# Bank evacuations one step later in a 16-wide attention, and one turn inside a run of value products in a 64-wide one

## The chip, the cores and the metric

The kernel runs on one core of a Trainium2 chip. The metric is the time of one execution on the device, in microseconds; lower is better. A core has a matrix engine (TensorE, PE in the rows), three engines for elementwise work (VectorE or DVE, ScalarE or ACT, GpSimd or POOL), a queue that issues transfers (SP), and a PSUM memory of eight banks into which TensorE writes. Every engine works through its own instructions in the order in which they are written; semaphores hold one engine back until another has done its part.

## The reference

Two layers on 2048 tokens (4 sequences of 512) of width 256, in fp32:

```python
x = x + linear_attention(layernorm(x))          # 16 heads, decaying
x = x + hadamard_ffn(layernorm(x))              # gated, 1024 wide
x = x + attention16(layernorm(x))               # 16 heads of 16, 4 key heads, rope
x = x + attention64_and_experts(layernorm(x))   # 32 heads of 64, causal; then 16 experts, top 4
```

The change touches the third and the fourth line. In both the attention is `softmax(q k^T) v` with rotated queries and keys. The third line, for one sequence n:

```python
q, k, v = x @ Wq.T, x @ Wk.T, x @ Wv.T     # 16 query heads, 4 key and value heads, width 16
q, k = q*cos + rotate_half(q)*sin, k*cos + rotate_half(k)*sin
out = softmax(q @ k.T * 16**-0.5) @ v      # every head on its own
x = x + out @ Wo.T
```

## The kernel before, in words

The order of the work on every engine is written out by hand. The 16-wide attention (the functions called `narrow`) is one loop over numbered steps, `for slot in range(FIRST_SLOT, END_SLOT)`, from -38 to 136, that each engine walks by itself. In a step s of 0 to 127 TensorE first makes two score tiles (L1842, two products of 64x512), then the scores of step s+12 for the maxima (L1855), in odd steps from 3 on the value products (L1867, 8 instructions), then whatever needs bank 6, the only bank for side work (`N_MBANK`). ScalarE begins a step with the two exponentials of that step's score tiles (L1451, 128x512 each); TensorE may write the score tiles of step s+1 once the first exponential of step s is done. VectorE takes the negated maxima (L1079, two a step) and adds them, transposed, into the queries (L1097).

The preparations make the queries and keys of the next sequence, in 4 tiles of 128 tokens, for sequences 1 to 3 beside the steps above; those of sequence 0 run from step -38 on, when there is nothing else. `prepared_at(slot, offset)` says which tile is due: tile t of sequence n starts at step 32n - 38 + 5t, and the offset counts from there. All of these use bank 6 one after the other:

- offset 0: TensorE projects the tile (L1909); ScalarE copies it out (L1484, "the projection's copy").
- offset 1: rope on GpSimd (on VectorE for sequence 0), L499 to L503.
- offset 3: ScalarE writes the high halves (L1462 and L1463, four instructions, "the high parts"), then GpSimd or VectorE the rests.
- offsets 6, 7, 8: TensorE turns the keys and then twice four query tiles (L1898, "the turns"); ScalarE copies each out (L1474: 256 columns for the keys, 512 for the queries).

Before each use of bank 6 TensorE waits (`pe.wait_ge(*emptied)`) until the use before it has been copied out. A next tile starts 5 steps later, so offset 5 of a tile is offset 0 of the next, and its offset 8 is offset 3 of the next. The bank also takes the transposes of the maxima (L1876, in steps 6 and 7 of every 8) and the output projection (L1887, steps 37 and 39 of every 32).

The 64-wide attention runs 32 rounds of 16 slots. The table `WIDE` says what follows a slot's scores (L1773): `turn` transposes probabilities (L1783; VectorE copies the even ones out, ScalarE the odd ones, L1419), `values` multiplies by the values (L1795; after step 3 ScalarE copies the result, L1432), `turn_qk` turns the next round's queries (even numbers, 4 tiles, copied at L1398 to `wide_q`) or keys (odd, 2 tiles, to `wide_k`) in bank 6, and `high` and `low` split them. TensorE waits before a `turn_qk` until the one before has been copied out. ScalarE holds a slot's exponential (L1406) back until the next `turn` or `values` of the table.

Of the kernel before, what the change touches and what calls it, by code (L numbers as in the profile page):

```python
# [74 lines left out]
def two_layers(nc, x_in, slope, W_qkvu, W_out0, SU_ug, SU_dp, Wscale_ug, Wscale_dp, W_up, W_gate, W_down,  # L75
               Wq1, Wk1, Wv1, Wo1, ln_w, ff_ln_w, wq, wk, wv, wo, wg, w1, w3, w2, consts, out):
    ctx = ExitStack()
    with ctx:
# [192 lines left out]
        def n_probs(pair):  # L271

            ring = most_probs[:, 2 * (pair % 6):2 * (pair % 6) + 2, :] if pair % 6 < 4 else \
                more_probs[:, 2 * (pair % 6) - 8:2 * (pair % 6) - 6, :]
            return ring
# [84 lines left out]
        def prepared_at(slot, offset):  # L360

            for n in range(B):
                t, rest = divmod(slot - 32 * n - FIRST_SLOT - offset, 5)
                if rest == 0 and 0 <= t < TB:
                    return n, t
            return None

        def projected_at(slot, offset):
# [13 lines left out]
                9: [("turn_qk", 1, 2), ("turn", 0, 2), ("high", 1, 2), ("qkv", 1, 3)],  # L382
                10: [("low", 1, 2), ("turn_qk", 1, 3), ("turn", 0, 3)],
                11: [("turn", 0, 4), ("high", 1, 3)],
                12: [("low", 1, 3), ("turn", 0, 5), ("values", 0, 0), ("values", 0, 1), ("values", 0, 2), ("values", 0, 3),
                     ("turn_qk", 1, 4)],
                13: [("turn", 0, 6), ("turn_qk", 1, 5)],
                14: [("turn_qk", 1, 6), ("project", 0, 0)],
                15: [("turn_qk", 1, 7), ("values", 0, 4), ("values", 0, 5), ("values", 0, 6), ("turn", 0, 7)]}
# [123 lines left out]
        def narrow_parts(t):  # L513

            whole = n_t1[:, t % 2, :]
            q = whole[:, 0:D].rearrange("p (g i d) -> p i g d", g=KV16, i=4)
            k = whole[:, D:320].rearrange("p (g d) -> p g d", g=KV16)
            qx = n_x[:, t % 2, 0:8, :].rearrange("p (i k) (e w d) -> p i (k e) w d", k=2, e=2, w=4)
            kx = n_x[:, t % 2, 8:10, :].rearrange("p k (e w d) -> p (k e) w d", e=2, w=4)
            return q, k, qx, kx  # L520
# [730 lines left out]
        def _(act):  # L1251
# [191 lines left out]
            def narrow():  # L1443

                for slot in range(FIRST_SLOT, END_SLOT):
                    if 0 <= slot < 8 * SETS:
                        act.wait_ge(n1["sT"], slot + 1)
                        if slot >= 6:
                            act.wait_ge(n1["pv"], (slot - 6) // 2 + 1)
                        for e in range(2):  # L1450
                            nc.scalar.activation(n_probs(slot)[:, e, :], bank[(2 * slot + e) % 3], ACT.Exp).then_inc(n1["exp"], 1)  # L1451
                    at = prepared_at(slot, 3)
                    if at:
                        n, t = at
                        m = TB * n + t
                        q, k, qx, kx = narrow_parts(t)
                        act.wait_ge(n1["sum"], m + 1)
                        act.wait_ge(n1["fill"], 6)
                        if m >= 2:
                            act.wait_ge(n1["turn"], 3 * (m - 1))  # L1460
                        for w in range(2):
                            nc.scalar.activation(kx[:, :, 2 * w, :], k, ACT.Copy)  # L1462
                            ins = nc.scalar.activation(qx[:, :, :, w, :], q, ACT.Copy)  # L1463
                        ins.then_inc(n1["hi"], 1)
                    for i in range(3):
                        at = prepared_at(slot, 6 + i)
                        if at:
                            n, t = at
                            act.wait_ge(n1["turn"], 3 * (TB * n + t) + i + 1)
                            if n >= 2 and t == 0:  # L1470
                                act.wait_ge(n1["sT"], 32 * (n - 1))
                            tiles = n_q[:, n % 2, 4 * (i - 1):4 * i, P * t:P * t + P] if i else n_k[:, n % 2, :, P * t:P * t + P]
                            count = 4 if i else 2
                            nc.scalar.activation(tiles, bank[N_MBANK][:, 0:count * P].rearrange("p (k n) -> p k n", k=count), ACT.Copy,  # L1474
                                                 scale=HD16 ** -0.5 if i else 1.0).then_inc(n1["turned"], 1)
                    at = prepared_at(slot, 0)
                    if at:
                        n, t = at
                        m = TB * n + t
                        act.wait_ge(n1["qkv"], m + 1)  # L1480
                        if m >= 2:
                            act.wait_ge(n1["sum"], m - 1)
                            act.wait_ge(n1["v"], m - 1)
                        nc.scalar.activation(n_qkv[:, t % 2, :], bank[N_MBANK][:, 0:QKV], ACT.Copy).then_inc(n1["q_sb"], 1)  # L1484
# [3 lines left out]


            narrow()  # L1490

            for phase in (3, 4):
# [574 lines left out]
```

## Time and profile before

| | us |
|---|---|
| median of 3 runs | 2081.49 (2073.62 to 2081.84) |
| profiled execution | 2081.78 |
| its span, first to last instruction | 2080.0 |
| TensorE busy in the span | 1802.4 (87%) |
| VectorE busy | 1295.1 (62%) |
| ScalarE busy | 1069.6 (51%) |
| GpSimd busy | 904.0 (43%) |

The mean granted TensorE clock is 0.93 of full speed. The 16-wide attention runs from about 418 to 764 us, its steps 0 to 127 from 479.9 to about 750 us; the 64-wide one, with its rounds, from about 800 to 1709 us. Busy shares are averages over such stages, so the change has to be read inside its own stage. An idle time in a row stands in brackets, with the instruction whose end released it.

### The profile page before, as it was taken

How to read it: one execution, taken by the hardware profiler on the slowest of the kernel's cores; microseconds unless marked ns; L12 is line 12 of the kernel's file. 1: busy time of each engine (PE TensorE's matmuls, PEld its weight loads, DVE VectorE, ACT ScalarE, POOL GpSimd, SP SyncE). 2: the span in 40 equal slices, each digit the busy share in tenths (PEclk: the TensorE clock that was granted, in tenths of full speed). 3: DMA queues.
4: the chain of work that ended last, by engine and by line, in shares of the span. 5: the costliest groups of instructions: out<-in, count | busy, mean ns of one | idle time of the engine just before them, and what ended most of it. 6: DMA issues, size and time to landing. Idle time of an engine off the chain costs nothing.

```text
span 2080.0 us, 32302 instructions
## 1 busy us (share of the span) xinstructions
PE 1802.4 (87%) x10666; PEld 1222.2 (59%) x10666; DVE 1295.1 (62%) x3898; ACT 1069.6 (51%) x2854; POOL 904.0 (43%) x1013
## 2 busy tenths in 40 slices
PE   4999899957888855999999999999999984799994
PEld 2656688823334323776676667776766754555552
DVE  5775545446786855777777777777777766522222
ACT  3333344325565533666666666666666651344442
POOL 3992000003222001555555555555555551588884
PEclk9999899957999986999999999999999995899997
DMA  5000020000001010000000000000000008155556
GB/s 154 1 1 1 2 61 1 1 0 1 1 1 41 1 44 1 1 1 2 1 1 1 1 1 1 1 1 1 1 1 1 1 1 310 49 82 83 84 83 165
DMA packets 61426, 61.71 MB, mean 30 GB/s; under 512 B 13136, under 2 KB 58320, under 8 KB 61264
## 3 DMA queue, kind: packets, MB, share of 16 engines
q0 software_dynamic: 15360, 20.98, 6.3%
q1 hardware_dynamic: 45904, 38.65, 5.7%
q8 instruction: 91, 1.49, 0.3%
q14 instruction: 71, 0.58, 0.1%
HBM read 40.48 MB, written 19.14 MB: 29 GB/s over the span
## 4 chain that ended last, share of the span: by engine, by line
PE 55%; DVE 22%; issue 8%; ACT 8%; POOL 4%; DMA 2%; SPq 0%; POOLq 0%; ACTq 0%; DVEq 0%
PE banks L1813 6%; PE banks L1804 5%; PE banks L1773 4%; PE banks L1795 4%; PE banks L1783 4%; DVE con L1079 3%; PE banks L1990 3%; DVE wide_x L1052 3%; PE banks L1617 3%; PE banks L1825 2%; POOL wdT L725 2%; PE banks L1867 2%; PE banks L1679 2%; PE banks L1909 2%; DVE wugT L1037 2%
## 5 line engine op out<-in xcount | busy, mean ns | idle before, releaser
L1773 PE MATMUL banks<-wide_k,wide_q 128*128 128x512 f32 (+3 forms) x1024 | 308.3, 383 | 3.9 <-DVE con L1037 1.2
L1406 ACT ACTIVATE wugT<-wugT,con 128x512 f32<-128x512 f32 (+1 forms) x256 | 170.2, 666 | 137.5 <-DVE con L1037 137.4
L657 POOL TENSOR_TENSOR wugT<-wugT,con 128x512 f32<-128x512 f32 (+1 forms) x256 | 232.8, 935 | 2.5 <-DVE con L1016 2.5
L668 POOL TENSOR_TENSOR attn<-attn 128x320 f32<-128x320 f32 x128 | 111.5, 871 | 250.5 <-DVE attn L1004 250.5
L1037 DVE CUSTOM_DVE_ANT_0 wugT<-banks,wide_mask 128x512 f32<-128x512 f32 (+1 forms) x256 | 157.6, 616 | 98.8 <-PE banks L1773 94.9
L1773 PEld LDWEIGHTS banks<-wide_k,wide_q 128*128 128x128 f32 x1024 | 167.6, 191 | 59.4 <-DVE con L1037 23.5
L1813 PE MATMUL banks<-late,attn 128*128 128x384 f32 x512 | 191.6, 498 | 2.0 <-DVE attn L1009 1.2
L1079 DVE TENSOR_REDUCE con<-banks 128x1 f32<-128x512 f32 x256 | 163.8, 681 | 45.5 <-PE banks L1855 45.3
L1795 PE MATMUL banks<-attn 128*64 128x256 f32 x1280 | 166.4, 389 | 0.0
L1990 PE MATMUL banks<-w,late 128*128 x320 | 156.5, 612 | 2.5 <-ACT late L1529 1.7
L1237 DVE TENSOR_TENSOR late<-late,banks 128x256 f32<-128x256 f32 x80 | 33.7, 421 | 196.0 <-ACT late L1539 180.7
L1052 DVE TENSOR_TENSOR wide_x<-attn,wide_x 128x256 fp32r<-128x256 f32 (+1 forms) x256 | 134.1, 562 | 29.5 <-ACT wide_x L1436 29.5
L1825 PE MATMUL banks<-ident_r,wide_x 128*128 128x128 f32 x768 | 111.1, 255 | 39.5 <-ACT wide_q L1398 19.8
L1804 PE MATMUL banks<-late,attn 128*128 128x256 f32 x512 | 137.1, 390 | 6.5 <-ACT attn L1432 6.5
L739 POOL DMA_INDIRECT y_rows<-xnT,scatter_at x80 | 127.0, 1588 | 34.6 <-issue 22.2
L1783 PE MATMUL banks<-con,wugT 128*128 128x128 f32 x896 | 138.5, 277 | 0.1
L657 POOL TENSOR_TENSOR attn<-attn,con 128x128 f32<-128x128 f32 x128 | 50.0, 401 | 181.0 <-DVE con L1016 181.0
L1825 PEld LDWEIGHTS banks<-ident_r,wide_x 128*128 128x128 f32 x768 | 84.9, 141 | 70.9 <-ACT wide_q L1398 28.2
L1419 ACT ACTIVATE attn<-banks 128x512 f32<-128x512 f32 x160 | 94.6, 592 | 49.7 <-PE banks L1783 49.7
L1813 PEld LDWEIGHTS banks<-late,attn 128*128 128x128 f32 x512 | 93.3, 194 | 41.0 <-issue 2.4
L1804 PEld LDWEIGHTS banks<-late,attn 128*128 128x128 f32 x512 | 91.8, 190 | 39.6 <-ACT attn L1432 16.9
L1041 DVE COPY attn<-banks 128x512 f32<-128x512 f32 x160 | 109.4, 684 | 6.6 <-PE banks L1783 6.6
(310 smaller groups left out, 4155.5 us busy)
## 6 DMA issues: line engine op xcount, KB each, us to landing
w<-in_L_ffn_w_dram SPq DMA_DIRECT2D x32, 256.0 KB, 5.6
late<-in_L_ffn_w_dram SPq DMA_DIRECT2D x16, 256.0 KB, 6.2
y_rows<-wqkv1T SPq DMA_DIRECT2D x1, 2176.0 KB, 7.9
x<-in_L_attn_x_dram SPq DMA_DIRECT2D x4, 512.0 KB, 9.0
late<-in_L_ffn_wq_dram SPq DMA_DIRECT2D x2, 1024.0 KB, 7.3
late<-in_L_ffn_wo_dram SPq DMA_DIRECT2D x1, 2048.0 KB, 9.1
h_rows<-wugT SPq DMA_DIRECT2D x1, 2048.0 KB, 7.0
y_rows<-x SPq DMA_DIRECT2D x1, 2048.0 KB, 12.8
```

The lines of the kernel that those rows point to most:

```text
L657: nc.gpsimd.tensor_tensor(p, p, rinv[:, m:m + 1].to_broadcast([P, n]), ALU.mult).then_inc(at.sem["norm"], 1)
L1037: nc.vector.tensor_tensor_reduce(at.prob(a)[:, 0:kk], sc, wide_mask[:, S - kk:S], -1.0, 3.0e38, ALU.add, ALU.min, negmax[:, a:a + 1]).then ...
L1052: ins = nc.vector.tensor_tensor(dst(1), whole, high, ALU.subtract)
L1079: nc.vector.tensor_reduce(n_max[:, s % 4, j // 4, j % 4, e:e + 1], bank[3 + (2 * pair + e) % 3], AX, ALU.max, negate=True).then_inc(n1["ma ...
L1406: nc.scalar.activation(at.prob(m)[:, 0:n], at.prob(m)[:, 0:n], ACT.Exp, bias=negmax[:, m:m + 1], scale=-1.0, accum_out=rowsum[:, m:m + 1]) ...
L1773: ins = nc.tensor.matmul(sbank[:, 0:keys], wide_q[:, side, i, qcols], wide_k[:, side, w, 0:keys], start=(w == 0), stop=(w == 1))
L1783: ins = nc.tensor.transpose(bank[PTBANK[a % 2]][:, P * i:P * i + P], at.prob(4 * q + i)[:, P * k:P * k + P], ident)
L1795: ins = nc.tensor.matmul(bank[OBANK][HD64 * e:HD64 * e + HD64, 0:D], wide_v[:, side, k, :], pT.rearrange("p (c e n) -> p e c n", e=2, n=P) ...
L1804: ins = nc.tensor.matmul(at.ybank("project", a)[:, 0:D], at.onT[:, a % ring, P * c:P * c + P], w_out(n, c), start=(c == 0), stop=(c == chu ...
L1813: ins = nc.tensor.matmul(at.ybank("qkv", a)[:, 0:QKV], wide_xT[:, c, first:first + P], w_qkv(n, c), start=(c == 0), stop=(c == DC - 1))
L1825: ins = nc.tensor.transpose(bank[MBANK][:, P * h:P * h + P].bitcast(F32R), src[:, t % 2, z + P * h:z + P * h + P], ident_r[:])
L1990: ins = nc.tensor.matmul(bank[j % 2], m_xT[:, j % 2, c, :], w13[:, bass.ds(e, 1), c, :, :].rearrange("p e i d -> p (e i d)"), start=(c == ...
```

## The change

Two places. In ScalarE's loop of the 16-wide attention the offset of the copies of bank 6 grows by one: the turns' copies (L1474) from 6, 7, 8 to 7, 8, 9, and the projection's copy (L1484) from 0 to 1. TensorE's order there stays. In the table of the 64-wide attention, `turn_qk` 4 stands between the values 1 and 2 instead of behind the values 3.

```diff
-                12: [("low", 1, 3), ("turn", 0, 5), ("values", 0, 0), ("values", 0, 1), ("values", 0, 2), ("values", 0, 3),
-                     ("turn_qk", 1, 4)],
+                12: [("low", 1, 3), ("turn", 0, 5), ("values", 0, 0), ("values", 0, 1), ("turn_qk", 1, 4), ("values", 0, 2),
+                     ("values", 0, 3)],
...
                     for i in range(3):
-                        at = prepared_at(slot, 6 + i)
+                        at = prepared_at(slot, 7 + i)
                         if at:
...
-                    at = prepared_at(slot, 0)
+                    at = prepared_at(slot, 1)
                     if at:
```

ScalarE's instructions in steps 31 to 34 before, where sequence 2 begins to be prepared beside the attention of sequence 1 (`attn1` is the projected tile, `banks3` holds bank 6, `wugT` and `wdT` the exponentials; `banks0` and `banks1` hold the score tiles):

```order
L1484 ACTIVATE attn1<-banks3 128x384
L1451 ACTIVATE wugT<-banks0 128x512
L1451 ACTIVATE wugT<-banks1 128x512
L1474 ACTIVATE narrow_k<-banks3 128x2x128
L1451 ACTIVATE wugT<-banks0 128x512 x2
L1474 ACTIVATE narrow_q<-banks3 128x4x128
L1451 ACTIVATE wdT<-banks1 128x512
L1451 ACTIVATE wdT<-banks0 128x512
L1462 ACTIVATE narrow_x<-attn1 128x4x16
L1463 ACTIVATE narrow_x<-attn1 128x16x16
```

and of the same work in the changed kernel:

```order
L1451 ACTIVATE wugT<-banks0 128x512 x2
L1451 ACTIVATE wugT<-banks1 128x512
L1484 ACTIVATE attn1<-banks3 128x384
L1451 ACTIVATE wugT<-banks0 128x512 x2
L1474 ACTIVATE narrow_k<-banks3 128x2x128
L1451 ACTIVATE wdT<-banks1 128x512
L1451 ACTIVATE wdT<-banks0 128x512
L1462 ACTIVATE narrow_x<-attn1 128x4x16
L1463 ACTIVATE narrow_x<-attn1 128x16x16
L1462 ACTIVATE narrow_x<-attn1 128x4x16
L1463 ACTIVATE narrow_x<-attn1 128x16x16
L1474 ACTIVATE narrow_q<-banks3 128x4x128
```

Each copy has moved behind two exponentials, and the first copy of the queries also behind the four instructions of the high parts.

TensorE in slots 12 and 13 of a round of the 64-wide attention, as a difference (`banks3` holds bank 6):

```order
 L1773 MATMUL banks0<-wide_k,wide_q 128x128 x2
 L1783 MATMUL banks2<-con,wugT 128x128 x4
-L1795 MATMUL banks2<-attn2 64x256 x8
-L1825 MATMUL banks3<-ident_r,wide_x 128x128 x4
+L1795 MATMUL banks2<-attn2 64x256 x4
+L1825 MATMUL banks3<-ident_r,wide_x 128x128 x4
+L1795 MATMUL banks2<-attn2 64x256 x4
```

The four transposes of `turn_qk` 4 stand in the middle of the eight value products. ScalarE, which follows the same table, now copies the turned queries (L1398) before the values' result (L1432) instead of after it.

## Rows read from the trace of the kernel before

**Rows 1.** stages; us, busy of each engine (instructions), granted clock
```profile
480.00:764.00 284.00, 239.59 (x1408) 110.28 (x1408) 200.17 (x348) 170.50 (x349) 53.70 (x95) 0.96 0.05 16
```

**Rows 2.** timeline, steps 32 to 35; start, length, engine, line, what, [idle, releaser]
```profile
547.48 0.51 PE L1842 MATMUL banks<-narrow_q,narrow_k 64*128 64x512 f32 x2
...
547.59 0.49 ACT L1484 ACTIVATE attn<-banks 128x384 f32<-128x384 f32 x1 [3.34 <-PE banks L1909]
...
548.03 1.09 ACT L1451 ACTIVATE wugT<-banks 128x512 f32<-128x512 f32 x2
...
548.77 0.50 PE L1842 MATMUL banks<-narrow_q,narrow_k 64*128 64x512 f32 x2 [0.21 <-ACT wugT L1451]
...
549.00 0.39 ACT L1474 ACTIVATE narrow_k<-banks 128x256 fp32r<-128x256 f32 x1
...
550.43 0.54 PE L1898 MATMUL banks<-ident_r,narrow_x 128*128 128x128 f32 x4
...
550.89 0.50 PE L1842 MATMUL banks<-narrow_q,narrow_k 64*128 64x512 f32 x2
...
551.74 0.51 PE L1898 MATMUL banks<-ident_r,narrow_x 128*128 128x128 f32 x4
...
552.18 0.50 PE L1842 MATMUL banks<-narrow_q,narrow_k 64*128 64x512 f32 x2
...
552.45 0.27 ACT L1462 ACTIVATE narrow_x<-attn 128x64 fp32r<-128x64 f32 x1
...
553.35 0.60 ACT L1474 ACTIVATE narrow_q<-banks 128x512 fp32r<-128x512 f32 x1
...
554.50 0.50 PE L1842 MATMUL banks<-narrow_q,narrow_k 64*128 64x512 f32 x2 [0.59 <-ACT wdT L1451]
```

**Rows 3.** timeline, steps 6 and 7, the bank shared with the maxima
```profile
492.08 0.50 PE L1842 MATMUL banks<-narrow_q,narrow_k 64*128 64x512 f32 x2
...
492.74 0.54 PE L1876 MATMUL banks<-ident_r,narrow_mx 128*128 128x128 f32 x4
...
494.06 0.68 DVE L1097 TENSOR_TENSOR narrow_q<-narrow_q,banks 128x512 fp32r<-128x512 f32 x1
...
494.88 0.51 PE L1898 MATMUL banks<-ident_r,narrow_x 128*128 128x128 f32 x4 [1.61 <-DVE narrow_q L1097]
```

**Rows 4.** timeline, steps 0 and 1, the first exponentials
```profile
480.50 1.28 ACT L1451 ACT_TABLE_LOAD   x1
...
482.54 0.50 PE L1842 MATMUL banks<-narrow_q,narrow_k 64*128 64x512 f32 x2 [1.32 <-ACT wugT L1451]
```

**Rows 5.** timeline, sequence 0's preparations, tile 2
```profile
439.69 0.49 DVE L503 TENSOR_TENSOR attn<-attn 128x320 f32<-128x320 f32 x1
...
440.60 0.60 ACT L1474 ACTIVATE narrow_q<-banks 128x512 fp32r<-128x512 f32 x1 [0.90 <-PE banks L1898]
...
441.34 0.72 PE L1898 MATMUL banks<-ident_r,narrow_x 128*128 128x128 f32 x4 [0.78 <-ACT narrow_q L1474]
...
442.10 0.60 ACT L1474 ACTIVATE narrow_q<-banks 128x512 fp32r<-128x512 f32 x1
```

**Rows 6.** timeline, 64-wide attention, slots 13 and 14 of one round
```profile
1205.20 0.59 ACT L1398 ACTIVATE wide_q<-banks 128x512 fp32r<-128x512 f32 x1
...
1205.85 0.37 PE L1825 MATMUL banks<-ident_r,wide_x 128*128 128x128 f32 x2 [0.53 <-ACT wide_q L1398]
...
1205.97 0.20 ACT L1406 ACTIVATION_READ_ACCUMULATOR attn<-attn,con 128x1 f32 x1
...
1206.25 0.38 ACT L1398 ACTIVATE wide_k<-banks 128x256 fp32r<-128x256 f32 x1
```

**Rows 7.** waits from 820 to 1690 us; total us, times, longest
```profile
PE banks L1825 <- ACT wide_k L1398: 10.1, 31, 0.3
```

**Rows 8.** stages of 4 us around a long wait of TensorE
```profile
562.00:566.00 4.00, 1.53 (x12) 0.99 (x11) 2.57 (x4) 1.47 (x3) 0.00 (x0) 0.99 0.00 0
566.00:570.00 4.00, 4.00 (x20) 1.59 (x20) 1.29 (x2) 2.58 (x7) 0.49 (x2) 0.58 0.01 4
```

## The prediction

> **What bounds the kernel now.** I read the table of stages first, then the timeline of the stretch that the change touches, then the waits. In the stage of the 16-wide attention's steps TensorE is busy 239.6 of 284 us, VectorE 200.2 and ScalarE 170.5 [rows 1]. No engine fills it: TensorE, ScalarE and VectorE hand small buffers to each other, and one step lasts what the slowest of these hand-overs takes. The timeline shows which. Steps 32, 33 and 34 begin, by TensorE's score tiles (L1842), at 547.48, 548.77 and 550.89, step 35 at 552.18 and step 36 at 554.50 [rows 2]. The reader is to see that in steps 32 to 34 ScalarE copies bank 6 out in the gap in which TensorE is already making the next score tiles: the keys' copy starts at 549.00, 0.23 us after step 33 began, and when TensorE comes to its next turn at 550.43 the copy is long done. In step 35 the opposite: two copies, the exponentials of step 34 and the high parts in one row make ScalarE late, and TensorE idles 0.59 us before step 36. That is what the change goes for. In the 64-wide attention the same view shows TensorE idle 0.53 us before `turn_qk` 5, released by ScalarE's copy to `wide_q` [rows 6], and the waits show 31 waits for the following copy to `wide_k`, 10.1 us in all [rows 7].
>
> **16-wide attention, the steps beside preparations.** TensorE's order stays, and before a turn it still waits for the copy of the use before. That copy is now behind this step's two exponentials, and these wait for this step's score tiles. So in each step with a turn there is one chain on the path, counted from the step's start. The exponentials start 0.55 us in (548.03 against 547.48); the pair occupies ScalarE 0.97 us (548.03 to 549.00) [rows 2]; then comes the copy, 0.49 us for the projection, 0.39 for the keys, 0.60 for queries [rows 2]; TensorE starts 0.14 us after a copy's end (441.34 against 440.60 + 0.60) [rows 5]; the four transposes take 0.44 to 0.46 until the next step (551.74 to 552.18, 550.43 to 550.89) [rows 2], the two of the keys I take at 0.30.
> - Turn 0 (waits for the next tile's projection): 0.55 + 0.97 + 0.49 + 0.14 + 0.30 = 2.45 us; step 32 has 1.29.
> - Turn 1 (waits for the keys' copy): 0.55 + 0.97 + 0.39 + 0.14 + 0.46 = 2.51; step 33 has 2.12.
> - Turn 2 (waits for the first queries' copy, which is also behind the high parts, 0.90 us from 552.45 to 553.35): 0.55 + 0.97 + 0.90 + 0.60 + 0.14 + 0.44 = 3.60; step 34 has 1.29.
> - Step 35 gains: nothing holds its exponentials any more, so it takes what TensorE needs, 0.66 for two pairs of scores (492.08 to 492.74) [rows 3] and 1.00 for the value products (549.43, which is 548.77 + 0.66, to 550.43): 1.66 for 2.32.
>
> Together 8.56 for 4.70, less 0.66: +3.2 us for such a tile. Nothing covers it. The scores for the maxima stand before the turn in TensorE's queue, but the next step's scores, the maxima that VectorE takes of them and the next exponentials are all queued behind the waiting turn.
>
> The 12 tiles of sequences 1 to 3, by kind: (a) five like this one, the first tiles of sequences 2 and 3 and the third tiles of all three: 16.0 us. (b) The second tiles, where the transposes of the maxima and a VectorE addition stand between. In step 6 the transposes start 0.66 us in; behind the keys' copy they would start at 2.05, and the addition, which now starts 1.98 us in because VectorE first takes its maxima, at about 2.60: +0.6 instead of +1.4, the rest is under VectorE [rows 3]. With +0.5 for turn 0 and +1.5 for step 7, where the high parts count too but the step is long, 2.5 for sequence 1, and 1.6 each for sequences 2 and 3, whose steps 37 to 39 hold the output projection: 5.8. (c) The fourth tiles have no next projection and no high parts: 1.29 to 2.51 and 2.12 to 0.55 + 0.97 + 0.60 + 0.14 + 0.44 = 2.70, +1.8; in sequence 1 the second of these steps is already longer: 4.8 for three. (d) The first tile of sequence 1, steps 0 to 2: steps 1 and 2 lose 1.3 and 1.9. In step 0 the load of the exponential's table (1.28 us, today after the projection's copy, with TensorE idle 1.32 us behind it) [rows 4] comes directly behind the high parts of several us earlier and is free, but the first turn then waits for two exponentials and the copy, so the step only comes out even, +0.1: 3.3. (e) In the first tiles of sequences 2 and 3 the rope starts a step later and the high parts just miss it: 0.4 each, 0.8. Sum 30.7 us.
>
> For the table load the Trainium skill ("ScalarE: Activation LUTs", section "What ACT_TABLE_LOAD costs") adds a drain of about 1.4 us to the 1.28. The row shows 1.28 and TensorE going on at 482.54, with no room for it; by the page the sum would be 1.4 us lower.
>
> **Sequence 0's preparations.** There are no exponentials, but the first copy of the queries falls behind the high parts of the next tile, which wait for the rope. In tile 2 the rope ends at 440.18 (439.69 + 0.49) and the copy runs at 440.60 today, so that TensorE's second query turn starts at 441.34 [rows 5]. After: high parts at 440.22, 1.0 us long (the copies of 440.60 and 442.10 are 1.50 apart, of which the first takes 0.5 and the high parts between them the rest), copy at 441.21, turn at 441.95, +0.6. Three tiles: +1.9.
>
> **64-wide attention.** TensorE's four transposes move ahead of four value products, on an engine that waits 0.53 us soon after; free. ScalarE copies the queries before the values' result, 0.26 us earlier, so `turn_qk` 5 starts at about 1205.6 instead of 1205.85 and is over at 1206.0. The next copy (`wide_k`) can then follow the accumulator read of 1205.97 at once, at about 1206.06 instead of 1206.25 [rows 6]: TensorE's next turn, the end of this chain, comes 0.19 us earlier, in the 31 rounds that prepare a next one [rows 7]: -5.9 us. At worst it is nothing, or two more changes of operand at 0.04 us a round, +2.5. I take -5, near the rows.
>
> **The clock.** Where TensorE worked only 1.53 of 4 us the next 4 us had a granted clock of 0.58 and TensorE was busy all of them [rows 8]: part of them at 1.2 GHz instead of 2.4. Such a dip costs up to 4 x 0.42 = 1.7 us. After, steps 32 to 34 hold about 4.2 us of TensorE work in 8.6, and step 34 1.1 in 3.6, which is near that row. Bounds: no new dip (0) and one in each of the 12 groups (20). I take five, +8. The Trainium skill ("TensorE: Matmul & The Clock Gate", Part 1) has the half rate as the state that idleness restores; by that rule nearly every group would dip, which is the third rival below.
>
> **Sum.** 2081.8 (the profiled execution, 0.3 above the median) + 30.7 + 1.9 - 5 + 8 = 2117 us.
>
> **Rivals.**
> - *The exponentials were the bound* (the other side). If ScalarE's copies before the exponentials are what sets the steps, getting them out of the way wins 0.66 in each of the five steps like 35, the 1.3 of the table load and the 5.9 of the rounds: 2081.8 - 3.3 - 1.3 - 5.9 = 2071. It decides if TensorE's turn isn't late in spite of the order, that is if exponentials start less than 0.2 us into a step. Against it: they need that step's score tiles, 0.55 us in [rows 2]. 5%.
> - *VectorE covers half.* VectorE is at 70% of the stage [rows 1]; if it sets the pace around the turns as it does in step 6 [rows 3], only some of the stalls show: half of 30.7 and no dips, 2081.8 + 15.4 + 1.9 - 5 = 2094. Against it: VectorE follows steps of 1.29 us today [rows 2], and 2.45 and 3.60 are far beyond. 13%.
> - *The clock falls in every group*: 20 instead of 8, 2129. For it the rows 8, against it that the stage keeps 0.96 on the whole although it has waits of 1 to 2 us [rows 1, 3]. 12%.
> - *Nothing happens*: ScalarE idles 40% of the stage, and the order of its work is without effect; 2082. Against it the chain above. 5%.
>
> **How the numbers follow.** The forecast has 65%, with 2105 to 2129 as its own range. The range for 8 in 10 takes in the lower rival and the clock: 2095 to 2132. A measurement of this kernel tells 0.5%, about 10.4 us, from no change, so slower means above 2092 and faster below 2071. Slower: 65 + 12, and 9 of the 13 of the covered case: 86%. Same: the other 4, the 5 of no effect and 2 of the first rival: 11%. Faster: 3%.
>
> **What would show it.** Right: ScalarE's copies at L1474 are waited for by TensorE at L1898, some 1 to 2 us each, where there is hardly such a wait now; the start of step 33 is 2.4 to 2.5 us behind that of step 32, step 35 3.6 behind step 34, step 36 only 1.7 behind 35; the stage of the steps lasts about 315 to 325 us; a round of the 64-wide attention is 0.2 us shorter. Wrong: if TensorE's turns start at once after the scores, the chain isn't there; if steps are long but the granted clock stays at 0.96, the clock's term is; if the rounds keep their length, the copy to `wide_k` was held by something else.

## The result and the profile after

The changed kernel takes 2126.53 us (median of 4 runs, 2118.19 to 2130.71), the kernel before 2081.17 in the same session: a ratio of 1.0212 [1.0186, 1.0238], 2.1% slower. 2117 was forecast, and 2126.53 lies inside the forecast's own range of 2105 to 2129. One correction to the text above: the side bank of the 16-wide attention (`N_MBANK`) is bank 7, not 6. Bank 6 holds the value products there, and it is the side bank of the 64-wide attention. The argument does not depend on the number. The quoted expectations repeat the slip.

Stages of the two profiled executions, cut at the first instruction of a line:

| from to | before, us | after, us | difference | forecast |
|---|---|---|---|---|
| start to first projection (L1909) | 424.2 | 427.1 | +2.9 | 0 |
| to step 0 (L1842) | 55.7 | 57.0 | +1.3 | +1.9 |
| steps 0 to 127 | 268.7 | 318.5 | +49.8 | +38.7 (30.7 chain, 8 clock) |
| to the first 64-wide score (L1773) | 70.6 | 71.4 | +0.8 | 0 |
| 64-wide, first to last score | 880.8 | 874.5 | -6.3 | -5 |
| rest | 380.0 | 378.1 | -1.9 | 0 |

The first row lies ahead of everything that the change touches; it runs from 422.1 to 428.8 us in the profiled executions of this document. The 16-wide steps carry the result. The stage row of after, with the columns of [rows 1] (span; TensorE, its weight loads, VectorE, ScalarE, GpSimd; granted clock, DMA share, GB/s), and then the same for before with these cuts:

```profile
484.10:802.60 318.50, 249.20 (x1361) 109.34 (x1360) 200.88 (x343) 166.21 (x345) 52.59 (x93) 0.88 0.02 7
```

```profile
479.90:748.60 268.70, 228.21 (x1359) 102.88 (x1358) 197.59 (x343) 167.66 (x346) 52.83 (x93) 0.96 0.03 9
```

As many instructions as before, and VectorE, ScalarE and GpSimd as long at work. TensorE is busy 21 us longer on the same matmuls, at a granted clock of 0.88 for 0.96, and the rest is waiting. A single stage is not exact: another execution with the same 16-wide code (the first experiment below) took 312.1 us for these steps. Steps 32 to 36 of after, which answer to [rows 2]:

```profile
566.96 0.50 PE L1842 MATMUL banks<-narrow_q,narrow_k 64*128 64x512 f32 x2
...
567.50 1.08 ACT L1451 ACTIVATE wugT<-banks 128x512 f32<-128x512 f32 x2 [3.77 <-PE banks L1842]
...
568.48 0.50 ACT L1484 ACTIVATE attn<-banks 128x384 f32<-128x384 f32 x1
...
569.12 0.34 PE L1898 MATMUL banks<-ident_r,narrow_x 128*128 128x128 f32 x2 [1.42 <-ACT attn L1484]
...
569.38 0.50 PE L1842 MATMUL banks<-narrow_q,narrow_k 64*128 64x512 f32 x2
...
571.43 0.51 PE L1898 MATMUL banks<-ident_r,narrow_x 128*128 128x128 f32 x4 [0.32 <-ACT narrow_k L1474]
...
571.87 0.50 PE L1842 MATMUL banks<-narrow_q,narrow_k 64*128 64x512 f32 x2
...
572.41 1.08 ACT L1451 ACTIVATE wdT<-banks 128x512 f32<-128x512 f32 x2 [1.12 <-PE banks L1842]
...
573.38 0.26 ACT L1462 ACTIVATE narrow_x<-attn 128x64 fp32r<-128x64 f32 x1
...
574.28 0.59 ACT L1474 ACTIVATE narrow_q<-banks 128x512 fp32r<-128x512 f32 x1
...
575.02 0.72 PE L1898 MATMUL banks<-ident_r,narrow_x 128*128 128x128 f32 x4 [2.42 <-ACT narrow_q L1474]
...
575.67 0.79 PE L1842 MATMUL banks<-narrow_q,narrow_k 64*128 64x512 f32 x2
...
578.58 0.51 PE L1842 MATMUL banks<-narrow_q,narrow_k 64*128 64x512 f32 x2
```

The reader is to follow step 34. It begins at 571.87; its exponentials start 0.54 us later, because they need its score tiles; 0.97 later come the high parts, 0.90 long, then the copy of the queries (574.28), and only then TensorE's turn, at 575.02, after 2.42 us of idling. Steps 32 to 34 last 2.42, 2.49 and 3.80 us, before 1.29, 2.12 and 1.29 [rows 2].

The waits of after in the steps (waiting line <- releaser: total us, times, longest). None of these five rows exists in the kernel before:

```profile
PE banks L1898 <- ACT narrow_q L1474: 14.3, 6, 2.4
...
PE banks L1898 <- ACT attn L1484: 8.8, 7, 1.4
...
PE banks L1898 <- ACT narrow_k L1474: 6.7, 9, 1.3
...
PE banks L1876 <- ACT narrow_k L1474: 3.9, 3, 1.3
...
PE banks L1876 <- ACT narrow_q L1474: 1.3, 3, 0.5
```

Together 35.0 us; a sixth new row, of L1887 for the copy of L1484, has 0.9. The second loss is in the last two rows of the timeline: step 35 (575.67) was to last 1.66 us and lasts 2.91, with the same score tiles now 0.79 long instead of 0.50. Steps 34 and 35 of after as stages, then the same two of before:

```profile
571.87:575.67 3.80, 1.38 (x9) 0.86 (x8) 1.74 (x4) 2.47 (x7) 1.22 (x5) 0.91 0.00 0
575.67:578.58 2.91, 2.91 (x14) 0.70 (x13) 1.57 (x4) 1.57 (x3) 0.56 (x1) 0.53 0.02 6
```

```profile
550.89:552.18 1.29, 1.17 (x10) 0.70 (x10) 1.25 (x3) 1.18 (x3) 0.11 (x1) 1.00 0.00 0
552.18:554.50 2.32, 1.73 (x15) 0.53 (x14) 2.28 (x5) 2.32 (x8) 0.95 (x3) 1.00 0.03 7
```

TensorE worked 1.38 us in the 3.80 of step 34; in step 35 it is busy throughout at a granted 0.53, near its lower level of 1.2 GHz, where before it had 1.00 of 2.4 GHz. That is the pattern of [rows 8].

Step 0 of after, for [rows 4]. The table load is gone from here (it now runs at 476.51), but the first turn waits for the projection's copy, which is behind the exponentials:

```profile
484.93 1.08 ACT L1451 ACTIVATE wugT<-banks 128x512 f32<-128x512 f32 x2 [7.14 <-PE banks L1842]
...
485.90 0.50 ACT L1484 ACTIVATE attn<-banks 128x384 f32<-128x384 f32 x1
...
486.54 0.47 PE L1898 MATMUL banks<-ident_r,narrow_x 128*128 128x128 f32 x2 [1.23 <-ACT attn L1484]
```

Sequence 0's preparations, tile 2, for [rows 5]:

```profile
443.14 0.49 DVE L503 TENSOR_TENSOR attn<-attn 128x320 f32<-128x320 f32 x1
...
443.66 0.26 ACT L1462 ACTIVATE narrow_x<-attn 128x64 fp32r<-128x64 f32 x1 [0.65 <-PE banks L1898]
...
444.58 0.57 ACT L1474 ACTIVATE narrow_q<-banks 128x512 fp32r<-128x512 f32 x1
...
445.30 0.72 PE L1898 MATMUL banks<-ident_r,narrow_x 128*128 128x128 f32 x4 [1.64 <-DVE narrow_x L527]
```

The turn starts 1.67 us behind the rope's end (443.63), before 1.16 (441.34 - 440.18): +0.51. The row names VectorE as the releaser, but the turn comes 0.15 us behind the copy's end (445.15), so I read it as the copy's.

The 64-wide round: slots 12 to 14 of after, for [rows 6], and then two further rows of before that give the same distance.

```profile
1227.68 0.19 ACT L1406 ACTIVATION_READ_ACCUMULATOR wdT<-wdT,con 128x1 f32 x1
...
1229.14 0.58 ACT L1398 ACTIVATE wide_q<-banks 128x512 fp32r<-128x512 f32 x1
...
1229.62 0.37 ACT L1432 ACTIVATE attn<-banks 128x256 f32<-128x256 f32 x1
...
1230.27 0.38 ACT L1398 ACTIVATE wide_k<-banks 128x256 fp32r<-128x256 f32 x1
...
1230.79 0.50 PE L1825 MATMUL banks<-ident_r,wide_x 128*128 128x128 f32 x4 [0.41 <-ACT wide_k L1398]
```

```profile
1203.48 0.19 ACT L1406 ACTIVATION_READ_ACCUMULATOR wdT<-wdT,con 128x1 f32 x1
...
1206.78 0.51 PE L1825 MATMUL banks<-ident_r,wide_x 128*128 128x128 f32 x4 [0.33 <-ACT wide_k L1398]
```

The queries' copy now stands ahead of the values' result. From the accumulator read to the turn behind `wide_k` it is 3.11 us for 3.30: the 0.19 a round of the forecast.

### The profile page after: what moved, and what is told of

Read it like the earlier page. It is cut to its first block, busy times and chain, and to the rows that moved or that the text cites. A ratio compares the mean times of both kernels' runs of the same rounds, so it can differ in the third digit from the quotient of the medians.

```text
span 2126.6 us, 32302 instructions
## 1 busy us (share of the span) xinstructions
PE 1830.9 (86%) x10666; PEld 1226.6 (58%) x10666; DVE 1299.2 (61%) x3898; ACT 1065.6 (50%) x2854; POOL 902.8 (42%) x1013
## 4 chain that ended last, share of the span: by engine, by line
PE 54%; DVE 21%; ACT 9%; issue 9%; POOL 4%; DMA 1%; SPq 0%; ACTq 0%; POOLq 0%; DVEq 0%
PE banks L1813 6%; PE banks L1804 4%; PE banks L1773 4%; PE banks L1795 4%; PE banks L1783 4%; DVE wide_x L1052 3%; DVE con L1079 3%; PE banks L1990 3%; PE banks L1617 3%; POOL wdT L725 2%; PE banks L1842 2%; PE banks L1825 2%; PE banks L1867 2%; PE banks L1679 2%; PE banks L1887 2%
## 5 line engine op out<-in xcount | busy, mean ns | idle before, releaser
L1773 PE MATMUL banks<-wide_k,wide_q 128*128 128x512 f32 (+3 forms) x1024 | 308.9, 384 | 4.5 <-DVE con L1037 1.8
L1773 PEld LDWEIGHTS banks<-wide_k,wide_q 128*128 128x128 f32 x1024 | 167.2, 190 | 71.3 <-issue 24.8
L1795 PE MATMUL banks<-attn 128*64 128x256 f32 x1280 | 173.2, 392 | 0.0
L1451 ACT ACTIVATE wugT<-banks 128x512 f32<-128x512 f32 x172 | 93.4, 595 | 104.8 <-PE banks L1842 103.7
L1825 PE MATMUL banks<-ident_r,wide_x 128*128 128x128 f32 x768 | 111.4, 256 | 25.4 <-ACT wide_k L1398 12.7
L657 POOL TENSOR_TENSOR attn<-attn,con 128x128 f32<-128x128 f32 x128 | 49.8, 399 | 175.3 <-DVE con L1016 175.3
```

What stands on the lines that cost most here:

```text
L657: nc.gpsimd.tensor_tensor(p, p, rinv[:, m:m + 1].to_broadcast([P, n]), ALU.mult).then_inc(at.sem["norm"], 1)
L1773: ins = nc.tensor.matmul(sbank[:, 0:keys], wide_q[:, side, i, qcols], wide_k[:, side, w, 0:keys], start=(w == 0), stop=(w == 1))
L1795: ins = nc.tensor.matmul(bank[OBANK][HD64 * e:HD64 * e + HD64, 0:D], wide_v[:, side, k, :], pT.rearrange("p (c e n) -> p e c n", e=2, n=P) ...
L1825: ins = nc.tensor.transpose(bank[MBANK][:, P * h:P * h + P].bitcast(F32R), src[:, t % 2, z + P * h:z + P * h + P], ident_r[:])
```

## The experiments

Each is told with its median and its ratio to the kernel before, timed beside it in one of three sessions (the kernel before has 2081.05, 2081.04 and 2082.10 us in them). The ratio compares all runs of the two and isn't exactly the quotient of the medians. Compare kernels of different sessions by their ratios.

**The two halves apart.** First only the edits in ScalarE's 16-wide loop:

```diff
-                        at = prepared_at(slot, 6 + i)
+                        at = prepared_at(slot, 7 + i)
...
-                    at = prepared_at(slot, 0)
+                    at = prepared_at(slot, 1)
```

> Only the later copies of the 16-wide attention, the 64-wide table as before. Theory (bank chain plus clock): the whole loss and none of the gain, so the changed kernel's 2126.5 us plus about 6.3: 2133. Rival (the 64-wide edit is worth nothing, the two traces differ there for another reason): 2126 to 2127.

Measured: 2128.31 us, 1.0229 [1.0208, 1.0251]. That is 5 us under the 2133 that I had expected, about as far as the interval reaches. The steps take 312.1 us at a clock of 0.89, the 64-wide attention 880.9, as before. The whole loss is here. Then only the 64-wide table:

```diff
-                12: [("low", 1, 3), ("turn", 0, 5), ("values", 0, 0), ("values", 0, 1), ("values", 0, 2), ("values", 0, 3),
-                     ("turn_qk", 1, 4)],
+                12: [("low", 1, 3), ("turn", 0, 5), ("values", 0, 0), ("values", 0, 1), ("turn_qk", 1, 4), ("values", 0, 2),
+                     ("values", 0, 3)],
```

> Only turn_qk 4 between the values 1 and 2, the 16-wide attention as before. Theory: 0.20 us less in each of 31 rounds, 6.3 us in all: 2075. Rival (the rounds gain because what precedes them runs differently): no change, 2081.

Measured: 2074.93 us, 0.9965 [0.9950, 0.9980], and 872.7 us for the 64-wide attention. This half gains 6 us. The stage confirms it beyond its own scatter: the three profiled executions without this edit (the kernel before, the 16-wide half and the one with only the last copy later) take 878.8 to 880.9 us, the ten with ScalarE's new order 872.5 to 875.1. The two halves add up to +47.3 - 6.1 = +41 us, the whole change measured +45 in its own session; the difference is within the intervals of the ratios.

**Which engine's order gains in the 64-wide attention.** TensorE keeps the old table; only ScalarE takes `turn_qk` 4 ahead of the last values:

```diff
+                ops, moved = list(ops), ("turn_qk", 1, 4)
+                if moved in ops and ("values", 0, 2) in ops:
+                    ops.remove(moved)
+                    ops.insert(ops.index(("values", 0, 2)), moved)
                 act_work(a2, ops, it, par, wide_xT, sequence_of)
```

> 64-wide attention: TensorE's order as before (all four value products, then turn_qk 4), only ScalarE takes the copy of turn_qk 4 before the copy of the values' result; the 16-wide attention as before. Theory (ScalarE's order brings the gain): 6 us less, 2075, as with the whole 64-wide edit. Rival (TensorE's earlier transposes bring it): no change, 2081, with ScalarE idle before the copy until TensorE is done with four value products and the transposes.

Measured: 2075.37 us, 0.9978 [0.9964, 0.9992], 64-wide 872.5 us. The same as with both, so the gain is ScalarE's order, as the prediction had it; the turn's place among TensorE's value products is worth nothing that can be measured. One round of it (the line numbers are 4 higher in this kernel):

```profile
1198.17 0.19 ACT L1406 ACTIVATION_READ_ACCUMULATOR wdT<-wdT,con 128x1 f32 x1
...
1201.28 0.51 PE L1829 MATMUL banks<-ident_r,wide_x 128*128 128x128 f32 x4 [0.41 <-ACT wide_k L1398]
```

3.11 us again.

**Only the last copy later.** Steps like 35 lost 0.66 us in the old order, to a copy that stood ahead of the exponentials. Can that be had without the chain?

```diff
-                        at = prepared_at(slot, 6 + i)
+                        at = prepared_at(slot, (6, 7, 9)[i])
```

> Of the four copies of bank 6 in the 16-wide attention only the last one (the second four query tiles) is one step later, behind that step's exponentials; the bank's next user comes two steps after its turn, so TensorE should not wait for it. Theory: no new wait, and the steps 13, 35, 45, 67 and 77 (2.32 us) come down to about 1.7 since their exponentials start at once: 5 times 0.65, 3.3 us less: 2078. Rival (any copy behind the exponentials stalls the bank): 12 new waits of 0.5 to 1 us, 2088 to 2093.

Measured: 2081.58 us, 0.9997 [0.9983, 1.0011]: no gain that the runs can tell, and not the loss of the rival either. TensorE in steps 35 and 36 of it:

```profile
556.05 0.50 PE L1842 MATMUL banks<-narrow_q,narrow_k 64*128 64x512 f32 x2
...
557.88 0.50 PE L1842 MATMUL banks<-narrow_q,narrow_k 64*128 64x512 f32 x2
...
558.85 1.56 PE L1909 MATMUL banks<-wqkv1T,late 128*128 128x384 f32 x4 [0.24 <-ACT narrow_q L1474]
...
560.34 0.50 PE L1842 MATMUL banks<-narrow_q,narrow_k 64*128 64x512 f32 x2
```

Step 35 lasts 1.83 us for 2.32, but in step 36 the next user of the bank waits for the later copy, and that step lasts 2.46 for 2.15: 0.18 left of 0.49. Steps 67 and 68 do the same. In the three third tiles step 14 gives back 0.31 as well, but step 15 is 0.31 shorter (3.36 for 3.67), and 0.49 is left. That makes 1.8 us over the five tiles for the 3.3 expected, too little for these runs to tell from nothing. My expectation had looked at the step that gains and not at the next user of the bank.

**The clock.** If the clock falls because TensorE idles in the new waits, work in these waits must bring it back without touching the chain. Fillers are products whose result the next scores overwrite. Two versions of the changed kernel, with 1 to 10 fillers of 64x512 in the waiting steps; the second leaves them out of steps 0 to 2 and 17, where the clock is low anyway, and takes 4 for 5 in step 16. The diff is that of the first:

```diff
+                    idle = {0: 5, 1: 5, 2: 10, 5: 1, 6: 5, 7: 5, 10: 5, 11: 1, 12: 10, 16: 5, 17: 2, 32: 5, 33: 1, 34: 10, 37: 1, 38: 5, 39: 5, 42: 5, 43: 1, 44: 10, 48: 5, 49: 2, 64: 5, 65: 1, 66: 10, 69: 1, 70: 5, 71: 5, 74: 5, 75: 1, 76: 10, 80: 5, 81: 2}.get(slot, 0)
+                    if idle:
+                        pe.wait_ge(n1["max"], 2 * pair)
...
+                        for e in range(idle):
+                            nc.tensor.matmul(bank[3 + (2 * pair + 2) % 3], n_q[0:64, n % 2, 2 * i + k, P * t:P * t + P],
+                                             n_k[0:64, n % 2, k, :], start=True, stop=True)
```

> The changed kernel with filler products on TensorE: in the steps with a turn, behind the scores and the value products and before the wait for bank 6, 1 to 10 extra products of 64x512 (0.21 us each at 2.4 GHz) into the maxima's bank that is free at that moment; their results are overwritten and never read. They are sized to end before the copy they would wait for. Theory (the clock costs some 19 of the 50 us lost in the steps): the granted clock of the steps rises from 0.87 to 0.96 or more, the turns start where they did, and the time falls by 12 to 19 us, to 2108 to 2115. Rival (the low clock is only a mark of waiting and costs nothing): 2126, or a few us more for the added work.

Measured: 2112.21 us, 1.0143 [1.0113, 1.0174], within the 2108 to 2115 expected. But steps 0 to 2 grew from 9.9 to 13.8 us: TensorE is busy all of them at a granted 0.50, so there the fillers outlast the waits. So the second version:

> The changed kernel with the filler products of the earlier run, but only where TensorE had 2.4 GHz there: none in steps 0 to 4 and 17, 4 in step 16. Theory: the steps that follow a wait (13, 35, 45, 67, 77) take 1.66 us as worked out before the result, and the steps 0 to 127 about 303 us (310.5 with the ill-sized fillers, which cost 3.9 in steps 0 to 2 and some 3.5 in steps 17 to 22; 318.5 in the changed kernel): the time 2104 to 2108. Rival (the first filler run gained for another reason than the clock): no better than that run, 2112.

Measured: 2110.25 us, 1.0157 [1.0117, 1.0196]; the steps take 302.8 us, as expected, the whole some 2 us more than I had expected. The times don't tell the two versions apart, as the intervals overlap; the stage does, 310.6 and 302.8 us. Its stage, and its TensorE in steps 34 and 35:

```profile
481.60:784.40 302.80, 261.45 (x1490) 125.19 (x1489) 199.73 (x343) 166.16 (x345) 52.73 (x93) 0.95 0.02 8
```

```profile
567.76 0.50 PE L1842 MATMUL banks<-narrow_q,narrow_k 64*128 64x512 f32 x2
...
568.33 2.44 PE L1876 MATMUL banks<-narrow_k,narrow_q 64*128 64x512 f32 x10
...
570.91 0.51 PE L1906 MATMUL banks<-ident_r,narrow_x 128*128 128x128 f32 x4
571.35 0.50 PE L1842 MATMUL banks<-narrow_q,narrow_k 64*128 64x512 f32 x2
...
573.00 0.50 PE L1842 MATMUL banks<-narrow_q,narrow_k 64*128 64x512 f32 x2
```

Step 34 still lasts 3.59 us: the chain is untouched. Step 35 lasts 1.65 us instead of 2.91. So the clock's part is shown: more work on TensorE and the same chain, and the steps fall from 318.5 us (312.1 in the other execution of this order) to 302.8, and the time by some 11 us by the ratios. What remains, 302.8 against 268.7 at nearly the same clock (0.95 and 0.96), 34 us, is the chain and what low clock is left in steps 0 to 4, 7, 39 and 71.

**Parts of the chain.** Once the turns' copies ahead of the high parts, all else as in the changed kernel:

```diff
+                    for i in range(3):
+                        at = prepared_at(slot, 7 + i)
+                        if at:
...
+                            nc.scalar.activation(tiles, bank[N_MBANK][:, 0:count * P].rearrange("p (k n) -> p k n", k=count), ACT.Copy,
+                                                 scale=HD16 ** -0.5 if i else 1.0).then_inc(n1["turned"], 1)
                     at = prepared_at(slot, 3)
...
-                    for i in range(3):
-                        at = prepared_at(slot, 7 + i)
-                        if at:
...
```

> The changed kernel, but in ScalarE's step the copies of the turns come before the high parts instead of behind them. Theory: the second query turn starts 0.90 us earlier in the nine steps that hold high parts, and sequence 0's preparations get their 0.6 us three times back: 10 us, and 0 to 4 us more for the clock: 2113 to 2117. Rival (the step's length is set by something else than this chain): within 2 us of 2126.

Measured: 2105.89 us, 1.0113 [1.0080, 1.0146], 20.6 us less than the changed kernel. Steps 12 and 44 last 2.70 us, the 3.60 less the 0.90 of the high parts; the stage ahead of step 0 is back at 55.3 us. I had expected a smaller gain, 2113 to 2117 us. The shorter waits go with a higher clock (0.91, for 0.88), and TensorE is busy 239.5 us in the steps instead of 249.2; that this is the whole of the excess isn't shown. And once the projection's copy back in its old place:

```diff
-                    at = prepared_at(slot, 1)
+                    at = prepared_at(slot, 0)
```

> The changed kernel with the projection's copy back at offset 0, only the turns' copies one step later. Theory: the steps with the first turn of a tile lose their wait: 1.2 us in the five even ones, 0.5 in three odd ones, nothing at step 0, where the exponential's table is loaded late again: 7.6 us, and 0 to 3 for the clock: 2116 to 2119. Rival: within 2 us of 2126.

Measured: 2113.81 us, 1.0151 [1.0118, 1.0184], 12.7 us less, 2 more than the most that I had expected. Steps 10, 32, 42, 64 and 74 last 1.19 to 1.29 us again.

**What is worth keeping.** The gain of the 64-wide edit, the later last copy, and the exponential's table loaded early by an exponential of one column in step -1, when ScalarE is idle:

```diff
+                    if slot == -1:
+                        nc.scalar.activation(room[:, 0:1], const("left"), ACT.Exp, scale=0.0)
...
-                        at = prepared_at(slot, 6 + i)
+                        at = prepared_at(slot, (6, 7, 9)[i])
```

> The kernel before with three things: the 64-wide edit, only the last of the four copies one step later, and an exponential of one column before step -1, so that the exponential's table is loaded while ScalarE idles. Theory: 6.3 + 3.3 + 1.3 us less than before, 2070 to 2071. Rival (the steps are held by VectorE once the exponentials start earlier): only the 6.3, 2075.

Measured: 2071.72 us, 0.9955 [0.9937, 0.9973]. Steps 0 to 3 last 6.09 us together for 8.08. The early load alone is read against the version above with only the last copy later: steps 0 to 4 last 8.55 us for its 10.66. The runs give the whole gain as 9 us with an interval of 4 to either side, so they can't tell what the later copy adds.

**The clock in the old waits.** The kernel before has waits of TensorE too, for VectorE [rows 3]. On top of the version just told, 3 to 6 fillers stand in such waits (steps 6, 7, 15, 31, 37 to 39, 47 and so on). `filler(count, ...)` writes `count` products of 64x512 as above:

```diff
+                    filler({39: 3, 71: 3, 103: 4}.get(slot, 0), slot + LEAD)
...
+                    filler({6: 6, 7: 3, 15: 4, 37: 3, 38: 6, 39: 3, 47: 4, 69: 3, 70: 6, 71: 3, 79: 4}.get(slot, 0), slot + LEAD)
...
+                    filler({31: 4, 63: 4}.get(slot, 0), slot + LEAD)
```

> The best kernel so far (64-wide edit, last copy one step later, early table load) with 3 to 6 filler products of 64x512 in the waits for VectorE that the kernel before has too (steps 6, 7, 15, 31, 37 to 39, 47, 63, 69 to 71, 79, 103). Theory: the low clock in steps 7, 9, 39, 49, 71 and 81 (5.88 us instead of 3.2 in step 9, 3.2 to 3.4 instead of 2.1 in 49 and 81) goes with these waits and goes away: 5 to 9 us less than that kernel, 2063 to 2067. Rival (those dips come from the run itself, or the fillers lengthen what follows them): 2071 or more.

Measured: 2060.13 us, 0.9912 [0.9884, 0.9941]. The steps:

```profile
477.90:736.40 258.50, 237.52 (x1422) 110.35 (x1421) 197.25 (x343) 164.83 (x345) 52.75 (x93) 1.00 0.03 9
```

The version without these fillers had 269.8 us at 0.94. Step 9 lasts 3.15 us for 5.88, step 39 8.07 for 11.65. Last, transposes of the identity in the waits ahead of step 0 as well (`warm(count, bank)` writes `count` of them to a bank that is free there; a second `warm(5, 3)` stands before the projection):

```diff
+                    if -12 < slot < 0:
+                        warm(7, 0)
...
+                    if slot < -12 and any(prepared_at(slot, 6 + i) for i in range(3)):
+                        warm(5, 3)
```

> The same with transposes of the identity in the waits before step 0 too: 5 before each use of bank 6 in sequence 0's preparations and 7 in each of the steps -11 to -1, written to banks that are free there. Theory: where the granted clock is 0.50 to 0.57 from 422 to 480 us, it comes up, four projections fall from 2.93 to 1.49 us and steps -12 to 3 shorten: 6 to 12 us less than the kernel with the other fillers, 2053 to 2060. Rival (these waits are too short a part for the clock to come up): within 2 us of it, or slower by the added work.

Measured: 2056.05 us, 0.9895 [0.9865, 0.9925], the fastest of all, but 4 us less than without them where I had expected 6 to 12, and the intervals of the two overlap. The gain is seen in the stage. The one ahead of step 0 takes 50.3 us at a clock of 0.81, and 55.3 at 0.53 without:

```profile
422.10:472.40 50.30, 42.79 (x252) 29.42 (x250) 25.23 (x56) 14.54 (x39) 3.81 (x6) 0.81 0.00 1
```

```profile
422.60:477.90 55.30, 35.11 (x96) 17.17 (x96) 25.65 (x56) 14.97 (x39) 3.74 (x6) 0.53 0.00 0
```

## Why the prediction was right, and which term was too small

The mechanism held: TensorE waits at L1898 for the copies of L1474 and L1484, and the steps with a turn of a plain tile last 2.4 to 3.6 us at the full clock, as worked out. The clock's term did not hold, and a part of the agreement by kinds of tile is luck, as told below.

To part the chain from the clock I took each step's shortest length in the executions with the changed order (the changed kernel, the 16-wide half alone and the two with fillers) and in those with the old order (before and the two 64-wide experiments). Summed over the 127 step lengths this gives 297.0 and 265.2 us: the chain costs 31.9. The rest of the 49.8, 17.9 us, is steps with the same work that ran slower; 0.5 of it, in step 61, at a granted 1.00, so not for the clock.

The split is rough. A dip that every execution of an order has is counted as chain: step 71 lasts 10.97 us or more in the four executions of the changed order, at a granted 0.84 at best, and 8.07 at 1.00 in a later version with fillers in the old order; steps 0 to 2 run at 0.50. And the other execution of this 16-wide code has 6.4 us less, which leaves 11.5 for its clock. The version with fillers gives 34 for the chain and 16 for the clock.

- *The chain of a plain tile* held to 0.03 us: turns 2.42, 2.49 and 3.59 (forecast 2.45, 2.51, 3.60), the step behind them 1.66 (1.66). The five plain tiles cost 15.7 us (16.0).
- *Second tiles*, where VectorE's addition covers a part: 5.9 (5.8), with step 6 at +0.62 and step 7 at +1.46 (+0.6, +1.5). That the sum agrees is luck: it holds +1.58 for the dip of step 71 and -0.47 for step 9. *Fourth tiles*: 5.0 (4.8).
- *The first tile of sequence 1*: 4.7 (3.3). Step 0 came out even, +0.20 (+0.1), as the load of the table was freed and the first turn took its place. Steps 1 and 2 lost 1.8 and 2.4, not 1.3 and 1.9: step 1 begins with score tiles of 0.79 us, and the granted clock is 0.50 in both.
- *Late rope*: steps 29 and 61 +0.7 each in the changed kernel (0.4); in one version with fillers step 61 has only +0.2.
- *Sequence 0*: +0.51 in tile 2 (0.6); the stage +1.3 in the changed kernel and 1.0 to 1.6 in the three others with the same order there (1.9).
- *64-wide attention*: 0.19 a round as forecast; -6.3 us for -5. I had taken a little less than the 5.9 of the rows. ScalarE's order alone does it.
- *The clock* is the term that was mis-sized, near 18 us in the profiled execution (11 to 18 over the executions above) and not 8. I had allowed a dip in five of the twelve groups. In the changed kernel at least one step of each of the twelve groups runs over 0.25 us longer than its shortest (steps 4, 9, 13, 17, 35, 39, 45, 49, 67, 71, 77 and 81, one of each); in the kernel before only steps 17 and 71 do, against the two 64-wide experiments. That doesn't make the others of the old order free of dips: its step 9 has a granted 0.64 and its step 39 0.85, and with fillers in the old waits step 9 falls from 4.80 to 3.15 us and step 39 from 9.30 to 8.07.
- *The third rival*, at 12% and 20 us, described the clock better than the forecast did. My argument against it, that the old stage keeps 0.96 in spite of waits of 1 to 2 us, compared the waits that were there with three new ones in a row. It also set aside the prediction's own count, 1.1 us of work in the 3.6 of step 34, which stood near the row for which the clock had fallen; 1.38 in 3.80 were measured. Nothing in the rows spoke for five groups rather than twelve. The rule of the Trainium skill ("TensorE: Matmul & The Clock Gate", Part 1) that I had put beside it, by which idleness brings the half rate back, fits these runs better than my five did: a granted 0.53 in step 35 behind the waits, and 1.00 in the same step where fillers stood in them. The page speaks of idleness; here TensorE was at work for 1.38 of the 3.80 us, in pieces, before the clock fell.

The first two rivals and the fourth are out: exponentials start 0.54 us into the step and not earlier, and VectorE hides only what the second tiles already had. With 31.9 and 17.9 for 30.7 and 8 the sum would have been 2128.5, against a median of 2126.5 and 2129.0 for the profiled execution.

## What to carry to other kernels

When an evacuation is moved behind other work of its engine, write down the chain to the next user of that buffer, and price it from the rows: here the turns came to wait for score tiles, two exponentials and the copy, and steps of 1.2 to 2.2 us became steps of 2.4 to 3.6. Move a copy only when nobody waits for its buffer before the work that it steps back for is done, and look at the next user even where the step itself gains, as step 36 shows. Add the clock to the price of the waits that such a chain makes; here it was a third to more than half as much again.

## What the hardware showed that I had not expected

Useless products made the kernel faster. 3 to 6 of them in waits that the kernel already had, hardly on the path (steps 15, 47 and 79 grew by 0.17 us each), raised the granted clock of the steps from 0.94 to 1.00 and cut them from 269.8 to 258.5 us. The time fell from 0.9955 to 0.9912 of the kernel before, some 9 us. Where the granted clock stayed at 0.50 fillers hurt: ten of them lengthened step 2 from 4.10 to 6.09 us. The load of the exponential's table, 1.28 us in its row [rows 4], was worth 1.07 us in step 0 (2.65 to 1.58) and 2.1 in steps 0 to 4 together once it ran early.
